# A GNN layer on one core: VectorE's centring moved to the end of its round, odd gathers issued four batches ahead

## Chip, cores and metric

The kernel runs on one core of one Trainium2 chip. The metric is device time in microseconds (us) of one execution, lower is better. Three runs of the kernel before gave a median of 1585.3 us (1584.4 to 1585.63).

## What is computed

One message-passing layer over 100000 nodes of 64 features and 25000 edges, all in fp32. Cut to what matters:

```python
h = jnp.maximum(_layernorm(x, axis=-1), 0.0)
edge_in_f = concat([h[src], h[dst], edge_attr])           # 25000 x 192
msgs_f = relu(edge_in_f @ W1_f + b1_f) @ W2_f + b2_f      # 25000 x 128
agg = segment_sum(msgs_f, dst, n_nodes)
edge_in_r = concat([h[dst], h[src], edge_attr])
msgs_r = relu(edge_in_r @ W1_r + b1_r) @ W2_r + b2_r
agg = agg + segment_sum(msgs_r, src, n_nodes)
out = x + h + relu(concat([agg, h]) @ Wn1 + bn1) @ Wn2 + bn2
```

## The kernel before, in words

There are three stages. The **first** walks over the nodes in 98 windows, normalises them and writes h times a part of Wn1 to a table in HBM. The **third** walks over the same windows, reads the table back and finishes the node MLP. The change touches the **second**, the edge stage.

The edge stage walks over the edges in 98 batches of 256 edges, which have 512 ends, in four groups of 128. For one batch n the work is, in order of data:

- GpSimd *gathers* the rows of x for the four groups (`gather`, L523). Those of even batches are all fetched during the first stage. Those of odd batches go to a ring of four buffers `got_odd`; the first `LOOK` of them (L93) are fetched in the first stage, and the others during the edge stage by `gather_odd` (L543), two of the four groups after each scatter.
- VectorE sums and *centres* the rows (`centre`, L964, instructions at L978 and L980); ScalarE squares them (`square`, L614); VectorE sums the squares (`variance`, L1002); ScalarE takes the root (L619); VectorE scales (`normal`, L1033 and L1037) into `h_ends`.
- TensorE transposes (`turn`, L821 and L824), ScalarE copies the result out (`copy_turned`, L625 and L626), TensorE does `layer1` (L835, L837), ScalarE the `relu` (L633), TensorE `layer2` (L850), and VectorE adds a bias (`messages`, L1028).
- VectorE compares the ends of the batch with one another (`match`, L988 and L996) and works out where each row goes (`targets`, L1008 to L1015, and `aim`, L1022). TensorE sums the messages of equal ends by 20 matmuls (`join`, L863), ScalarE copies these sums out (`copy_sums`, L642).
- GpSimd *scatters* with addition: four indirect DMAs into the table (`scatter`, L541). A scatter starts only when the one before it has landed, when `aim` has written its addresses and when `copy_sums` has written its rows.

Every engine has its own program, a fixed list of steps that it does strictly one after the other; semaphores tie them together. A round n of an engine works on several batches at once. `w.do(f, -2)` means: do f for batch n-2. The lists of ScalarE and TensorE, which the diff leaves alone, are:

```python
# ScalarE, batch(w)
w.do(root)
w.do(relu, -1)
if not fill:
    h_window(w, range(G // 2))
w.do(square, 1)
w.do(copy_sums, -2)
w.do(copy_turned)
# TensorE, batch(w)
w.do(join, -2)
w.do(turn)
w.do(layer2, -1)
w.do(layer1)
```

ScalarE's list ends with the other half of `h_window` (L656), which recomputes h for one window of nodes, beside the edges. GpSimd's round is `scatter` of batch n, then `gather_odd`. `aim` (VectorE, batch n-2) waits until the scatter of batch n-4 has landed, since that scatter still reads the same addresses. The buffers of a step are two, by the parity of the batch.

Of the kernel before, what the change touches and what calls it, by code (L numbers as in the profile page):

```python
# [77 lines left out]
def gnn_layer(nc, x, src, dst, edge_attr, W1_f, b1_f, W2_f, b2_f, W1_r, b1_r, W2_r, b2_r, Wn1, bn1, Wn2, bn2, out):  # L78
# [11 lines left out]
    TB = NT // 2  # L90
    TAIL = E - (NT - 1) * P
    RING = 4
    LOOK = 3  # L93
    PAUSED = 190
    EARLY = 4
    assert NB % 2 == 0 and 0 < TAIL < P and TB < P
# [22 lines left out]
    with ExitStack() as ctx:  # L119
# [177 lines left out]
        def first(i):  # L297
            return isinstance(i, int) and i == 0
# [207 lines left out]
        def _(pool):  # L506
# [14 lines left out]
            def gather(to, numbers, landed, tiles=range(KB)):  # L521
                for k in tiles:
                    pool.indirect_dma_start(to[:, k * D:(k + 1) * D], None, x,  # L523
                                            bass.IndirectOffsetOnAxis(ap=numbers[:, k:k + 1], axis=0)
                                            ).then_inc(landed, 16)
# [18 lines left out]
            def gather_odd(w):  # L544


                pair = w.of(2, 2 * LOOK)[0]
                turn, place = w.of(2 * RING, 2 * LOOK)
                place //= 2
                half = w.n % 2  # L550
                if isinstance(pair, int) and pair < RING:
                    numbers = gather_first[:, (2 * pair + 1) * KB:(2 * pair + 2) * KB]
                else:
                    numbers = gather_at[place]
                    if half == 0:
                        pool.wait_ge(s_gat[place], turn)
                        pool.wait_ge(s_centred[1], pair - RING + 1)
                        pool.sem_inc(s_gathers_begun, 1)
                gather(got_odd[place][:, 0, :], numbers, s_got[place], range(half * JT, (half + 1) * JT))
# [4 lines left out]
            for b in range(NB):  # L564
# [7 lines left out]
                for k in range(KB):  # L572
                    if s == 0:
                        gather(got_even[:, i, :], at, s_got_even[i >= EARLY], [k])
                    elif i < LOOK:
                        gather(got_odd[i][:, 0, :], at, s_got[i], [k])
# [9 lines left out]
            def batch(w):  # L586
                w.do(scatter)
                if w.there(2 * LOOK):
                    gather_odd(w)
# [330 lines left out]
        def _(dve):  # L920
# [35 lines left out]
            def gather_rows(w):  # L956


                place = w.of(2 * RING, 2 * RING)[1] // 2
                dve.tensor_copy(gather_at[place][:, :], gather_first[:, bass.ds(w.number(2 * RING + 1) * KB, KB)]  # L960
                                ).then_inc(s_gat[place], 1)

            def centre(w, k):
                i, s = w.of(2, k)  # L964
                if s == 0:
                    rows = got_even[:, bass.ds(i, 1), :]
                    if first(i):
                        dve.wait_ge(s_got_even[0], 16 * KB * EARLY)
                    elif isinstance(i, int) and i == EARLY:
                        dve.wait_ge(s_got_even[1], 16 * KB * (PAIRS - EARLY))  # L970
                else:
                    turn, place = w.of(2 * RING, k)
                    rows = got_odd[place // 2][:, :, :]
                    dve.wait_ge(s_got[place // 2], 16 * KB * (turn + 1))
                rows = rows.rearrange("p a (k d) -> p (a k) d", d=D)
                if not first(i):
                    dve.wait_ge(s_h[s], i)
                dve.tensor_reduce(sums[s][:, :], rows, AX.X, ALU.add).then_inc(s_sums[s], 1)  # L978
                dve.wait_ge(s_sums[s], i + 1)
                dve.scalar_tensor_tensor(out=centred[s][:, :, :], in0=sums[s][:, :].to_broadcast([P, KB, D]),  # L980
                                         scalar=-1.0 / D, in1=rows, op0=ALU.mult, op1=ALU.add
                                         ).then_inc(s_centred[s], 1)
# [58 lines left out]
            def batch(w):  # L1041
                w.do(variance)
                w.do(aim, -2)
                if w.there(1):
                    centre(w, 1)
                w.do(match, -1)
                w.do(normal)
                if w.n % 2 == 0 and w.there(2 * RING):
                    gather_rows(w)
                w.do(targets, -1)  # L1050
                add_h(w, -1)
                w.do(messages, -1)

            def add_h(w, k):
                if not w.there(k):
                    return
                i, s = w.of(2, k)
                turn, place = w.of(NRING, k)
                dve.wait_ge(e_h[s], i + 1)
                if not in_ring(w, k):  # L1060
                    to = kept_slot(w, k)
                else:
                    to = nxh[place][:, :, :]
                    if not first(turn):
                        dve.wait_ge(e_stored[place], 16 * (turn - skipped(w, k)))
                dve.tensor_tensor(to, nx[place][:, :, :], nh[s][:, :, :], ALU.add).then_inc(e_xh[s], 1)
# [66 lines left out]
            for s in range(2):  # L1133
# [3 lines left out]
                                     in1=all_rstd[:, :, :], op0=ALU.mult, op1=ALU.mult).then_inc(e_means, 1)  # L1137
            assert 2 * EARLY == 8
            run(dve, NB, [(8, MORE_FROM * NRING, 2 * RING), (MORE_FROM * NRING, 88, 2 * RING)], 2, batch)


# [41 lines left out]
```

## Time and profile before

| | |
|---|---|
| median of three runs | 1585.3 us |
| the profiled execution, its own time | 1586.9 us |
| its span, from first to last instruction | 1585.2 us |
| busy: TensorE, VectorE, ScalarE, GpSimd | 1284.4, 972.0, 940.2, 1094.1 us |
| mean granted share of TensorE's full clock | 0.855 |
| first scatter starts, read of the table starts | 331.6 us, 1328.1 us |

The span is what the trace covers; the execution's own time is 1.7 us longer, and the median of the runs 1.6 us shorter than that. In the rows below PE is TensorE, DVE VectorE, ACT ScalarE, POOL GpSimd. A bracket at a row's end gives the idle time before it and what ended it; "issue" there is time in which the engine waited for nothing that the profile shows. The granted clock stands as a share of 2.4 GHz: 1.00 is 2.4 GHz, 0.50 is 1.2 GHz.

### The profile page before, as it was taken

The page shows a single profiled execution, that of the slowest core. Times are in us where ns is not written, and L with a number is a line of the kernel's source. Part 1 is how long each engine was busy: PE and PEld are TensorE (multiplying, and loading weights), DVE is VectorE, ACT ScalarE, POOL GpSimd, SP SyncE. Part 2 cuts the span into 40 slices and gives each one's busy share as a digit, 9 for nine tenths or more (in the row PEclk, how much of TensorE's full clock was granted, in tenths as well). Part 3 has the DMA queues.
Part 4 walks back from the last instruction along what each step waited for, and adds up shares of the span by engine and source line. Part 5 has one row for each costly group of instructions (what it writes and reads, how often), then busy time and mean ns, then how long its engine had stood idle before and what let it go on. Part 6 is the DMA issues. An engine that isn't in the chain of part 4 may idle for free.

```text
span 1585.2 us, 29464 instructions
## 1 busy us (share of the span) xinstructions
PE 1284.4 (81%) x7070; PEld 975.8 (62%) x7070; DVE 972.0 (61%) x3294; ACT 940.2 (59%) x2256; POOL 1094.1 (69%) x985
## 2 busy tenths in 40 slices
PE   5889988747778887787778888777778873999998
PEld 4677777535556666565556666656656652777776
DVE  7999999636666666666666666666666650222222
ACT  4888888635555555545455555555545532777776
POOL 8889878878888888888888888888888863000000
PEclk9999999778887778778887777878887776999999
DMA  6899998535555555555555555555555545999998
GB/s 201 296 315 313 315 313 304 173 60 110 105 110 110 110 105 106 105 105 106 105 99 103 103 103 106 106 105 104 100 104 96 101 91 153 382 371 370 365 363 298
DMA packets 238986, 281.00 MB, mean 177 GB/s; under 512 B 53746, under 2 KB 155776, under 8 KB 238924
## 3 DMA queue, kind: packets, MB, share of 16 engines
q1 hardware_dynamic: 168696, 241.57, 45.7%
q0 software_dynamic: 68992, 38.59, 19.9%
q14 instruction: 57, 0.47, 0.1%
q10 hardware_dynamic: 1236, 0.30, 0.1%
q8 instruction: 5, 0.08, 0.0%
HBM read 162.62 MB, written 117.72 MB: 177 GB/s over the span
## 4 chain that ended last, share of the span: by engine, by line
POOL 54%; issue 24%; PE 18%; DMA 2%; DVE 1%; POOLq 1%; ACT 0%; SPq 0%; DVEq 0%
POOL table L541 30%; POOL got_even L523 13%; POOL got_odd L523 7%; PE bank L888 6%; PE bank L899 6%; POOL to_send L583 4%; PE bank L909 3%; DMA table<-to_send,scatter_at 2%; PE bank L863 1%; PE bank L837 0%; PE bank L835 0%; DVE same L996 0%; PE bank L850 0%; DMA same<-table 0%; DMA gather_begin<-in_src 0%
## 5 line engine op out<-in xcount | busy, mean ns | idle before, releaser
L541 POOL DMA_INDIRECT table<-to_send,scatter_at x392 | 622.2, 1587 | 133.0 <-issue 117.1
L863 PEld LDWEIGHTS bank<-message,same 128*128 128x128 f32 x1960 | 272.3, 224 | 41.9 <-issue 39.5
L863 PE MATMUL bank<-message,same 128*128 128x128 f32 x1960 | 293.2, 315 | 2.2 <-DVE message L1028 2.2
L656 ACT ACTIVATE nh<-nx,all_sums,all_rstd 128x64 f32<-128x64 f32 x784 | 280.1, 433 | 0.0
L523 POOL DMA_INDIRECT got_even<-in_x,gather_first x192 | 207.4, 1080 | 37.7 <-issue 37.7
L821 PE MATMUL bank<-ident,h_ends 128*128 128x128 f32 x196 | 55.0, 376 | 218.0 <-DVE h_ends L1037 218.0
L792 PE MATMUL bank<-wn_h,nturned 128*128 128x256 f32 x784 | 196.0, 393 | 31.3 <-ACT nhidden L700 26.6
L523 POOL DMA_INDIRECT got_odd<-in_x,gather_at x180 | 179.9, 999 | 54.9 <-issue 54.9
L996 DVE TENSOR_SCALAR_CACHE_REDUCE same<-others,ids 128x128 f32<-128x128 int32 (+3 forms) x392 | 190.7, 543 | 12.7 <-DVE ids L988 11.0
L792 PEld LDWEIGHTS bank<-wn_h,nturned 128*128 128x128 f32 x784 | 142.7, 192 | 67.5 <-issue 34.8
L1022 DVE TENSOR_TENSOR scatter_at<-moved,ids 128x4 int32<-128x4 f32 x98 | 15.9, 162 | 265.4 <-DMA table<-to_send,scatter_at 265.4
L835 PE MATMUL bank<-turned,w_ends 128*128 128x256 f32 x392 | 166.8, 516 | 5.0 <-ACT turned_edge L626 5.0
L821 PEld LDWEIGHTS bank<-ident,h_ends 128*128 128x128 f32 x196 | 27.8, 184 | 231.0 <-issue 230.7
L633 ACT ACTIVATE hidden<-bank,b 128x256 f32<-128x256 f32 x196 | 82.0, 469 | 141.4 <-PE bank L837 141.4
L837 PE MATMUL bank<-turned_edge,w_edge 64*128 64x256 f32 x392 | 164.6, 506 | 0.0
L730 ACT ACTIVATE nhidden<-bank,bn_col 128x512 f32<-128x512 f32 x196 | 124.0, 683 | 56.6 <-PE bank L888 56.6
L625 ACT COPY turned<-bank 128x256 f32<-128x256 f32 x98 | 36.5, 373 | 194.3 <-PE bank L824 193.5
L850 PE MATMUL bank<-w2n,hidden 128*128 128x128 f32 x784 | 149.8, 355 | 0.0
L850 PEld LDWEIGHTS bank<-w2n,hidden 128*128 128x128 f32 x784 | 141.4, 269 | 2.1
L888 PE MATMUL bank<-ident,same 128*128 128x128 f32 x784 | 108.6, 282 | 26.0 <-DMA same<-table 25.7
L888 PEld LDWEIGHTS bank<-ident,same 128*128 128x128 f32 x784 | 85.7, 143 | 63.9 <-issue 62.2
L837 PEld LDWEIGHTS bank<-turned_edge,w_edge 64*128 64x128 f32 x392 | 69.2, 220 | 87.7 <-issue 87.7
(81 smaller groups left out, 2012.9 us busy)
## 6 DMA issues: line engine op xcount, KB each, us to landing
nx<-in_x SPq DMA_DIRECT2D x194, 256.0 KB
table<-nhidden SPq DMA_DIRECT2D x97, 512.0 KB
same<-table SPq DMA_DIRECT2D x97, 512.0 KB, 5.3
others<-numbers SPq DMA_DIRECT2D x196, 128.0 KB
out_x<-nh SPq DMA_DIRECT2D x79, 256.0 KB, 4.0
nx<-out_x SPq DMA_DIRECT2D x55, 256.0 KB, 4.3
out_x<-ncentred SPq DMA_DIRECT2D x49, 256.0 KB, 4.3
table<-to_send,scatter_at POOLq DMA_INDIRECT x392
```

The source lines that it names most:

```text
L523: pool.indirect_dma_start(to[:, k * D:(k + 1) * D], None, x, bass.IndirectOffsetOnAxis(ap=numbers[:, k:k + 1], axis=0)).then_inc(landed, 16)
L541: pool.indirect_dma_start(table, bass.IndirectOffsetOnAxis(ap=scatter_at[s][:, k:k + 1], axis=0), to_send[s][:, k, :], None, compute_op=AL ...
L656: last = act.activation(nh[s][:, g, :], nx[place][:, g, :], ACT.Relu, bias=all_sums[:, at, g:g + 1].rearrange("p a g -> p (a g)"), scale=a ...
L730: act.activation(nhidden[s][:, odd * 512:odd * 512 + 512], bank[2 + 2 * s + odd][:, :], ACT.Relu, bias=bn1_col[:, 0:1]).then_inc(n_hidden[ ...
L792: last = pe.matmul(bank[2 + 2 * s + half][:, c:c + 2 * M], nturned[s][:, q * P:(q + 1) * P], wn1_h[:, :, :].rearrange("p a m -> p (a m)"), ...
L835: pe.matmul(bank[2 + s][:, c:c + JT * P], w1_ends[:, end, :], turned[s][:, 0:JT * P], start=True, stop=False)
L837: last = pe.matmul(bank[2 + s][:, c:c + JT * P], w1_edge[:, end, :], turned_edge[s][:, :], start=False, stop=True)
L850: last = pe.matmul(bank[4 + s][:, k * M:(k + 1) * M], hidden[s][:, end, j * P:(j + 1) * P], w2n[:, end, :], start=True, stop=True)
L863: last = pe.matmul(bank[6 + s][:, k * M:(k + 1) * M], same[s][:, o, k * P:(k + 1) * P], message[s][:, o, :], start=(o == k), stop=(o == KB ...
L888: last = pe.transpose(bank[2 + 2 * s + odd][:, q * P:(q + 1) * P], ntab[place][:, g * M:(g + 1) * M], ident[:, :])
L899: last = pe.matmul(bank[s][odd * D:(odd + 1) * D, c:c + 256], wn2[:, :], nhidden[s][:, odd * 512 + c:odd * 512 + c + 256], start=True, sto ...
L996: last = dve.tensor_scalar(same[s][:, o, 0:w], row[:, 0:w], ids[s][:, o:o + 1], None, ALU.is_equal, ALU.add, accum_out=matches[s][:, o:o + 1])
```

## The change

Two edits. In VectorE's round, `centre` of batch n+1 stood right behind `aim`; it now stands at the end, behind `messages` of batch n-1, with `gather_rows` behind it. `gather_rows` copies the indices for a later odd gather to a place where GpSimd may read them. And `LOOK` is 2 instead of 3, so that in round n, with n even, GpSimd begins to gather odd batch n+5 and no longer n+7, and four gathers fewer are done in the first stage.

```diff
-    LOOK = 3
+    LOOK = 2
@@ VectorE
             def batch(w):
                 w.do(variance)
                 w.do(aim, -2)
-                if w.there(1):
-                    centre(w, 1)
                 w.do(match, -1)
                 w.do(normal)
-                if w.n % 2 == 0 and w.there(2 * RING):
-                    gather_rows(w)
                 w.do(targets, -1)
                 add_h(w, -1)
                 w.do(messages, -1)
+                if w.there(1):
+                    centre(w, 1)
+                if w.n % 2 == 0 and w.there(2 * RING):
+                    gather_rows(w)
```

VectorE in the middle of the edge stage, where one round ends and the next begins. L1028 is `messages` of n-1, L1002 `variance` and L1022 `aim` of the next round, L978 and L980 `centre`, L988 the start of `match`; the digit behind a name is its buffer. Before:

```order
L1066 TENSOR_TENSOR nh3<-nx1,nh1 128x512
L1028 TENSOR_TENSOR message1<-bank5,b2n 128x512
L1002 TENSOR_REDUCE var1<-squares1 128x4
L1022 TENSOR_TENSOR scatter_at1<-moved1,ids1 128x4
L978 TENSOR_REDUCE sums0<-got_even 128x4
L980 SCALAR_TENSOR_TENSOR centred0<-sums0,got_even 128x256
L988 COPY ids0<-ends_col 128x4
```

Now:

```order
L1066 TENSOR_TENSOR nh3<-nx1,nh1 128x512
L1028 TENSOR_TENSOR message1<-bank5,b2n 128x512
L978 TENSOR_REDUCE sums1<-got_odd1 128x4
L980 SCALAR_TENSOR_TENSOR centred1<-sums1,got_odd1 128x256
L960 COPY gather_at1<-gather_first 128x4
L1002 TENSOR_REDUCE var1<-squares1 128x4
L1022 TENSOR_TENSOR scatter_at1<-moved1,ids1 128x4
L988 COPY ids0<-ends_col 128x4
```

`centre` has moved ahead of `variance` and `aim` of the next round. Before, the batch that was centred was the one after the batch whose variance stood just ahead; now it is the same batch, with only ScalarE's `square` between them.

GpSimd where the first stage's gathers end and the scatters begin; x18 means 18 such instructions in a row. Before:

```order
L523 DMA got_even<-in_x,gather_first 128x64 x18
L541 DMA table<-to_send0,scatter_at0 100864x128 x4
L523 DMA got_odd3<-in_x,gather_first 128x64 x2
L541 DMA table<-to_send1,scatter_at1 100864x128 x4
L523 DMA got_odd3<-in_x,gather_first 128x64 x2
L541 DMA table<-to_send0,scatter_at0 100864x128 x4
L523 DMA got_odd0<-in_x,gather_at0 128x64 x2
```

Now:

```order
L523 DMA got_even<-in_x,gather_first 128x64 x14
L541 DMA table<-to_send0,scatter_at0 100864x128 x4
L523 DMA got_odd2<-in_x,gather_first 128x64 x2
L541 DMA table<-to_send1,scatter_at1 100864x128 x4
L523 DMA got_odd2<-in_x,gather_first 128x64 x2
L541 DMA table<-to_send0,scatter_at0 100864x128 x4
L523 DMA got_odd3<-in_x,gather_first 128x64 x2
```

Four gathers have left the run ahead of the first scatter, and every later pair of gathers is for an odd batch two batches nearer.

## Rows read from the trace of the kernel before

**Rows 1.** Busy us by stretch: PE, PEld, DVE, ACT, POOL; granted clock, DMA share, GB/s
```profile
341.00:1276.00 935.00, 740.19 (x3677) 566.44 (x3678) 602.08 (x2526) 485.58 (x1380) 766.70 (x551) 0.80 0.55 105
...
607.10:620.30 13.20, 12.13 (x44) 9.41 (x45) 9.17 (x43) 5.16 (x15) 10.76 (x9) 0.50 0.61 112
```

**Rows 2.** Timeline of GpSimd, one batch: start us, us, what
```profile
808.67 1.63 POOL L541 DMA_INDIRECT table<-to_send,scatter_at  x1 [0.30 <-issue]
...
816.22 1.02 POOL L523 DMA_INDIRECT got_odd<-in_x,gather_at  x1 [0.31 <-issue]
...
818.82 1.62 POOL L541 DMA_INDIRECT table<-to_send,scatter_at  x1 [0.30 <-issue]
```

**Rows 3.** Timeline of VectorE about the same time
```profile
804.26 0.69 DVE L1028 TENSOR_TENSOR message<-bank,b2n 128x512 f32<-128x512 f32 x1 [0.81 <-PE bank L850]
...
807.45 0.16 DVE L1022 TENSOR_TENSOR scatter_at<-moved,ids 128x4 int32<-128x4 f32 x1 [2.17 <-DMA table<-to_send,scatter_at]
807.53 0.42 DVE L978 TENSOR_REDUCE sums<-got_odd 128x4 f32<-128x256 f32 x1
807.98 0.42 DVE L980 SCALAR_TENSOR_TENSOR centred<-sums,got_odd 128x256 f32<-128x256 f32 x1
```

**Rows 4.** Timeline of ScalarE about the same time
```profile
808.99 0.41 ACT L614 ACTIVATE squares<-centred 128x256 f32<-128x256 f32 x1
809.44 0.58 ACT L642 COPY to_send<-bank 128x512 f32<-128x512 f32 x1
811.87 0.37 ACT L625 COPY turned<-bank 128x256 f32<-128x256 f32 x1 [1.84 <-PE bank L824]
812.14 0.36 ACT L626 COPY turned_edge<-bank 64x256 f32<-64x256 f32 x1
```

**Rows 5.** Timeline of TensorE, a batch at 2.4 GHz
```profile
811.20 0.41 PE L821 MATMUL bank<-ident,h_ends 128*128 128x128 f32 x2 [1.88 <-DVE h_ends L1037]
...
811.67 1.06 PE L850 MATMUL bank<-w2n,hidden 128*128 128x128 f32 x8
812.56 0.69 PE L835 MATMUL bank<-turned,w_ends 128*128 128x256 f32 x2
...
815.06 2.50 PE L863 MATMUL bank<-message,same 128*128 128x128 f32 x20
```

**Rows 6.** Timeline of TensorE, a batch at 1.2 GHz and the start of the next
```profile
609.05 1.92 PE L850 MATMUL bank<-w2n,hidden 128*128 128x128 f32 x8
610.76 1.06 PE L835 MATMUL bank<-turned,w_ends 128*128 128x256 f32 x2
...
615.20 4.63 PE L863 MATMUL bank<-message,same 128*128 128x128 f32 x20
619.62 0.63 PE L821 MATMUL bank<-ident,h_ends 128*128 128x128 f32 x2
...
620.48 1.08 PE L850 MATMUL bank<-w2n,hidden 128*128 128x128 f32 x8
```

**Rows 7.** Timeline of TensorE, two resumptions at 1.2 GHz behind a pause
```profile
309.91 1.22 PE L835 MATMUL bank<-turned,w_ends 128*128 128x256 f32 x2 [4.29 <-ACT turned_edge L626]
...
699.87 0.66 PE L821 MATMUL bank<-ident,h_ends 128*128 128x128 f32 x2 [2.89 <-DVE h_ends L1037]
```

**Rows 8.** Instructions and DMAs of the tile got_odd
```profile
DMA to landing us min/median/max: 2.3/2.5/5.8
```

**Rows 9.** Timeline of GpSimd: last early gather, first scatter, first scatter of batch 93
```profile
330.35 0.95 POOL L523 DMA_INDIRECT got_even<-in_x,gather_first  x1 [0.31 <-issue]
331.61 1.62 POOL L541 DMA_INDIRECT table<-to_send,scatter_at  x1 [0.30 <-issue]
...
1278.00 1.63 POOL L541 DMA_INDIRECT table<-to_send,scatter_at  x1 [2.62 <-DMA table<-to_send,scatter_at]
```

**Rows 10.** Timeline of VectorE: it reaches the wait for the first landing
```profile
340.54 0.16 DVE L1022 TENSOR_TENSOR scatter_at<-moved,ids 128x4 int32<-128x4 f32 x1 [18.47 <-DMA table<-to_send,scatter_at]
```

**Rows 11.** Who waited for whom, GpSimd, 341 to 1276 us: total us, times, longest
```profile
POOL table L541 <- ACT to_send L642: 0.9, 3, 0.3
```

## The prediction

> **What bounds the kernel now.** I read the engines by stretch first. In the edge stage, 341 to 1276 us, GpSimd is busy for 766.70 of 935 us and TensorE for 740.19, at a mean granted clock of 0.80 [rows 1]. So busy time alone doesn't tell who sets the pace; the waits do. GpSimd's timeline shows a batch of four scatters, from 808.67, and two gathers, from 816.22, and the next scatter at 818.82, 10.15 us after the first, with nothing ahead of it but 0.30 us of issue [rows 2]. Its waits in the whole stretch hold only 0.9 us for ScalarE's copy of the sums [rows 11]. So GpSimd's own list of instructions is the bound: from the first scatter at 331.61 to that of batch 93 at 1278.00 it makes (1278.00 - 331.61) / 93 = 10.18 us a batch [rows 9]. VectorE, ScalarE and TensorE run ahead and are held back at one place, VectorE's `aim`, which waits for a scatter to land: 2.17 us at 807.45 [rows 3].
>
> TensorE's work for one batch depends on its clock. At 2.4 GHz `layer1` takes 812.56 to 815.06 = 2.50 us, `join` 2.50, `turn` 811.20 to 811.67 = 0.47, `layer2` 1.06 [rows 5]: 6.53. At 1.2 GHz `layer1` takes 4.44 (610.76 to 615.20), `join` 4.42 (to the next turn at 619.62), `turn` 0.86, `layer2` 1.92 [rows 6]: 11.64, which is longer than GpSimd's batch. Today this does no harm: a low stretch as that of 607.10 to 620.30, with clock 0.50 [rows 1], is made up in the next batch. That the wait for ScalarE's copy shows up at all [rows 11] says that little is left over.
>
> **The change, part by part.** *Four gathers leave the start.* They stood in the run of unpaused gathers right ahead of the first scatter, 330.35 to 331.61 = 1.26 us each [rows 9]. The first scatter starts 4 x 1.26 = 5.0 us sooner, at 326.6. The same four come back in two more rounds of the edge stage, two each, 2.60 us [rows 2]; there they stand beside a wait for the landing that without them takes 2.62 us [rows 9]. That is 0 on the path, and if the cover were missing, 5.2 us. Sum: -5.0.
>
> *The copy of indices* (`gather_rows`, one small copy every second round) is moved with `centre`. GpSimd reads its result four rounds later instead of two, so its cost is nothing, covered by these rounds; uncovered it would be that small copy alone.
>
> *`centre` goes behind `messages`.* This adds no instruction, but it closes a ring. `messages` of batch m-1 waits for `layer2` of m-1. ScalarE's `square` of m+1 now waits for that, and behind `square` in ScalarE's fixed list stand `copy_sums` of m-2 and `copy_turned` of m. `layer1` of m needs `copy_turned` of m; in TensorE's list `join` of m-1, `turn` of m+1 and `layer2` of m follow, and `layer2` of m lets `messages` of m go. One turn of the ring is one batch, and nobody in it can run ahead. Before, `centre` needed nothing of TensorE's current batch, so `copy_turned` ran as soon as `turn` was done.
>
> Off TensorE the ring has: `messages` 0.69, `centre` 807.53 to 808.40 = 0.87 [rows 3], `square` to the start of the copy 0.45, `copy_sums` 0.58, `copy_turned` 811.87 to 812.50 = 0.63 [rows 4]. Sum 3.22. In this time TensorE does nothing. On TensorE the ring has all its work, in the order `layer1`, `join`, `turn`, `layer2`:
> - wholly at 2.4 GHz: 6.53 + 3.22 = 9.75 us, below GpSimd's 10.18;
> - wholly at 1.2 GHz: 11.64 + 3.22 = 14.86 us;
> - `layer1` and `join` at 1.2 GHz, `layer2` at 2.4: 4.44 + 4.42 + 1.06 + 3.22 = 13.14, and a `turn` of 0.47 to 0.86: 13.6 to 14.0.
>
> I take the third. The reason is the rows on the clock. TensorE resumed at 1.2 GHz after pauses of 2.89 and of 4.29 us [rows 7], and the new order puts a pause of 3.22 into each batch. The one at 309.91 is the new order's own case: the pause ended with `copy_turned`, and `layer1` came first. Once low, `layer1` and `join` stay low: in 24 batches of the trace the last three pairs of `layer1`'s matmuls ran at 1.2 GHz, and in 21 of these the whole `join` did; the clock rose in the next `turn` or `layer2`, as at 620.48 with 1.08 us instead of 1.92 [rows 6]. Before, `turn` and `layer2` came first after a pause and the clock was mostly back by `layer1`. Listed ends on one engine overlap the next start by some 0.1 us (0.37 listed, 0.27 to the next [rows 4]), so I take 13.7 and keep 13.3 to 14.0.
>
> *Odd gathers come two batches later.* Before, the rows of an odd batch were gathered ahead of one more batch of scatters (7.55 us [rows 2]) than the landing that `centre` stood behind, and were there in time. Now `centre` of odd batch m needs the second pair of gathers behind scatter m-4, and that scatter needs `copy_sums` of m-4, which ScalarE does right behind `square` of m-1. So from `centre` of m-1 to `centre` of m it takes at least: 0.87 + 0.45 + 0.58, scatters 808.67 to 816.22 = 7.55, one gather issued 1.30 (half of 2.60) [rows 2], and the second one's landing 2.5 [rows 8]: 13.25 us. The trace shows landings of 2.3 to 5.8 [rows 8], so the bounds are 13.05 and 16.55; the median is the nearest to a usual one. Even batches have no such wait. At 13.7 this is hidden behind the first ring, by only 0.45 us; a landing over 3.0 us would show.
>
> **The sum.** VectorE is free until its first wait for a landing [rows 10], which is `aim` of batch 2, in round 4. From round 4 to 96 are 93 rounds: 93 x (13.7 - 10.18) = 327.4 us. At the end GpSimd no longer trails its inputs by a batch, which gives back 0 to 10 us: -5. With the -5.0 from above: +317.4. The node stages have nothing changed. Against the profiled execution's own 1586.9 us this is 1904.3; the median of the runs shown is 1.6 lower: **1902.7, I say 1902 us**.
>
> **The rivals.** *The clock holds, the gathers bind* (0.22, with all mixtures up to 13.2 us a batch). If TensorE stays at 2.4 GHz, its ring of 9.75 is harmless, but odd batches take 13.25 and even ones 10.18: 11.7 on the mean. 93 x 1.54 = 143 us, less 5, from 1585.3: 1723 us. For it: TensorE would be busy for 6.53 of 9.75, and pauses of 1.88 us didn't lower the clock [rows 5]. Against it: 2.89 us did [rows 7], and 3.22 is longer.
>
> The Trainium skill's page "TensorE: Matmul & The Clock Gate", section "HAM oscillation — how this bites in real kernels", gives a length of idle gap up to which the clock isn't lowered, and 3.22 lies below it. By that rule this rival would be the outcome, 1723 us instead of 1902. The pause of 2.89 with 1.2 GHz behind it disagrees, so I leave it at 0.22.
>
> *All at 1.2 GHz, or late landings* (0.13). At 14.86 us a batch: 93 x 4.68 = 435, less 10: 2010 us; from 14.1 on it would be 1940. Against it: in the trace `layer2` was mostly back at 2.4 after a low `join`.
>
> *GpSimd keeps its pace* (0.05, of which 0.03 faster and 0.02 the same). If both rings close within 10.18 us, only the -5.0 is left: 1580.3 us, faster. The place is `centre` of the odd batches; the point from which it decides is a turn below 10.18, that is a landing some 3 us earlier than the 2.5 measured [rows 8] or rows fetched sooner than the code says, and a clock that holds. The order of GpSimd's instructions speaks against that.
>
> **How the numbers follow.** The forecast, 13.3 to 14.0 us a batch, 1865 to 1930 us, has 0.60. The range of 8 in 10 takes in most of the first rival, whose single value 1723 is its bottom, and the lower part of the second: 1720 to 1965. About 0.2% is what a measurement of this kernel can tell from no change; slower by more than that is 0.60 + 0.22 + 0.13 = 0.95, the same 0.02, faster 0.03.
>
> **What would show it.** In the changed kernel's profile: VectorE's wait of `aim` for the scatter's landing almost gone, and GpSimd waiting for ScalarE's `to_send`, some 3 us a batch; one pause a batch on TensorE, ahead of L835 and ended by `turned_edge`, of about 3.2 us, and none ahead of L821; granted clock in the edge stage near 0.65 instead of 0.80; L863 near 4.6 us in nearly every batch; the first scatter near 326.6. If instead the clock is high and GpSimd's scatters come 10.2 and 13.3 us apart in turn, the first rival holds. It is wrong altogether if the scatters keep 10.18 us.

## The result, and the profile after

The changed kernel took 1905.6 us (median of four runs, 1902.8 to 1906.4), the kernel before 1585.5 us beside it: a ratio of 1.2016 (95% interval 1.1995 to 1.2037), slower by 320 us. The prediction said 1902 us, with 1720 to 1965.

Of the changed kernel's page, the busy times, the granted clock in 40 slices, and the two costliest lines of GpSimd and TensorE:

```profile
span 1904.7 us, 29474 instructions
PE 1447.5 (76%) x7070; PEld 1089.5 (57%) x7070; DVE 975.1 (51%) x3294; ACT 923.7 (48%) x2256; POOL 1100.4 (58%) x985
...
PEclk9999996667766767676767676767666766799999
...
L541 POOL DMA_INDIRECT table<-to_send,scatter_at x392 | 629.4, 1606 | 447.5 <-ACT to_send L642 352.2
L835 PE MATMUL bank<-turned,w_ends 128*128 128x256 f32 x392 | 195.4, 592 | 381.1 <-ACT turned_edge L626 381.1
```

VectorE, ScalarE and GpSimd have the same work as before (1100.4 us of GpSimd against 1094.1); what is new is idle time. The scatters, which in [rows 2] waited for nothing but issue, now wait 352.2 us for ScalarE's copy of the sums. TensorE waits 381.1 us ahead of `layer1`.

The engines by stretch, columns as in [rows 1], and below it the longest waits in the same kernel, 500 to 1200 us (us in total, times, longest):

```profile
336.00:1590.00 1254.00, 888.40 (x3644) 670.09 (x3645) 600.68 (x2512) 464.40 (x1365) 773.60 (x552) 0.69 0.42 78
```

```profile
ACT squares L614 <- DVE centred L980: 310.1, 51, 7.9
DVE message L1028 <- PE bank L850: 263.2, 51, 5.9
...
PE bank L835 <- ACT turned_edge L626: 202.4, 52, 6.7
POOL table L541 <- ACT to_send L642: 192.8, 52, 4.7
...
DVE sums L978 <- DMA got_odd<-in_x,gather_at: 43.0, 26, 3.6
```

This is the ring, read off by its waits: `messages` waits for `layer2`, `square` for `centre`, `layer1` for `copy_turned`, each once a batch (51 or 52 times in 700 us). The wait of `aim` for a landing, 265.4 us in the kernel before by its page, is no longer in the list. The last line is the second ring, the wait of `centre` for a gather, every second batch. The mean granted clock in the edge stage fell from 0.80 to 0.69.

GpSimd's timeline, the first of the four scatters, at the stage's start, four times in its middle, and of batch 93:

```profile
324.58 1.63 POOL L541 DMA_INDIRECT table<-to_send,scatter_at  x1 [0.30 <-issue]
...
801.03 1.62 POOL L541 DMA_INDIRECT table<-to_send,scatter_at  x1 [3.05 <-ACT to_send L642]
...
814.97 1.63 POOL L541 DMA_INDIRECT table<-to_send,scatter_at  x1 [4.12 <-ACT to_send L642]
...
828.18 1.63 POOL L541 DMA_INDIRECT table<-to_send,scatter_at  x1 [2.87 <-ACT to_send L642]
...
1594.78 1.63 POOL L541 DMA_INDIRECT table<-to_send,scatter_at  x1 [4.24 <-ACT to_send L642]
```

From 324.58 to 1594.78 are 93 batches: 13.66 us each, against 10.18 before [rows 9]. The batches are not alike: the three scatters in the middle are 13.94 and 13.21 us apart. Over the stage the first scatter of an even batch comes 14.13 us behind that of the odd one before it, and that of an odd batch 13.20 us behind the even one's. Where the 319.5 us of span went: 1270.20 - 946.39 = 323.8 in these batches, -7.0 at the start (331.61 to 324.58), +2.7 behind batch 93.

TensorE in the same two turns of the ring, which are unlike in the same way:

```profile
800.62 0.70 PE L835 MATMUL bank<-turned,w_ends 128*128 128x256 f32 x2 [3.02 <-ACT turned_edge L626]
...
803.86 4.63 PE L863 MATMUL bank<-message,same 128*128 128x128 f32 x20
808.29 0.63 PE L821 MATMUL bank<-ident,h_ends 128*128 128x128 f32 x2
...
814.72 1.22 PE L835 MATMUL bank<-turned,w_ends 128*128 128x256 f32 x2 [4.56 <-ACT turned_edge L626]
...
819.32 4.10 PE L863 MATMUL bank<-message,same 128*128 128x128 f32 x20
823.26 0.38 PE L821 MATMUL bank<-ident,h_ends 128*128 128x128 f32 x2
...
827.77 0.70 PE L835 MATMUL bank<-turned,w_ends 128*128 128x256 f32 x2 [3.02 <-ACT turned_edge L626]
```

Behind a pause of 3.02 us `layer1` begins at 2.4 GHz (0.70 for a pair of matmuls) and the clock falls within it; behind 4.56 us it runs at 1.2 GHz from its start (1.22), and the clock is back before the join ends (4.10 instead of 4.63).

### The profile page after: what moved, and what is told of

The parts are those of the page before. It is cut to its first block, busy times and chain, and to the rows that moved or that the text cites. A ratio compares the mean times of both kernels' runs of the same rounds, so it can differ in the third digit from the quotient of the medians.

```text
span 1904.7 us, 29474 instructions
## 1 busy us (share of the span) xinstructions
PE 1447.5 (76%) x7070; PEld 1089.5 (57%) x7070; DVE 975.1 (51%) x3294; ACT 923.7 (48%) x2256; POOL 1100.4 (58%) x985
## 4 chain that ended last, share of the span: by engine, by line
PE 38%; issue 17%; POOL 17%; DVE 12%; DMA 9%; ACT 4%; ACTq 1%; DVEq 1%; SPq 1%; POOLq 0%
POOL table L541 14%; PE bank L863 10%; DMA got_odd<-in_x,gather_at 6%; PE bank L835 6%; PE bank L837 6%; PE bank L888 5%; PE bank L899 5%; DVE nvar L1087 3%; POOL got_odd L523 2%; PE bank L850 2%; PE bank L909 2%; DVE centred L980 2%; DVE sums L978 2%; DVE ncentred L1081 2%; ACT to_send L642 2%
## 5 line engine op out<-in xcount | busy, mean ns | idle before, releaser
L541 POOL DMA_INDIRECT table<-to_send,scatter_at x392 | 629.4, 1606 | 447.5 <-ACT to_send L642 352.2
L835 PE MATMUL bank<-turned,w_ends 128*128 128x256 f32 x392 | 195.4, 592 | 381.1 <-ACT turned_edge L626 381.1
L863 PEld LDWEIGHTS bank<-message,same 128*128 128x128 f32 x1960 | 399.4, 313 | 63.6 <-issue 62.7
L863 PE MATMUL bank<-message,same 128*128 128x128 f32 x1960 | 422.9, 407 | 0.8 <-DVE message L1028 0.8
L835 PEld LDWEIGHTS bank<-turned,w_ends 128*128 128x128 f32 x392 | 79.9, 254 | 449.4 <-ACT turned_edge L626 400.0
L614 ACT ACTIVATE squares<-centred 128x256 f32<-128x256 f32 x98 | 40.8, 416 | 589.5 <-DVE centred L980 589.5
L1028 DVE TENSOR_TENSOR message<-bank,b2n 128x512 f32<-128x512 f32 x98 | 67.7, 691 | 501.6 <-PE bank L850 501.6
L837 PE MATMUL bank<-turned_edge,w_edge 64*128 64x256 f32 x392 | 214.2, 643 | 0.0
L1008 DVE CUSTOM_DVE_ANT_0 junk<-same,from_here,matches 128x128 bf16<-128x128 f32 x392 | 114.0, 346 | 0.0
L850 PE MATMUL bank<-w2n,hidden 128*128 128x128 f32 x784 | 109.4, 284 | 0.0
L700 ACT COPY nhidden<-bank 128x512 f32<-128x512 f32 x196 | 105.3, 593 | 7.4 <-DMA table<-nhidden 7.3
```

What stands on the lines that cost most here:

```text
L541: pool.indirect_dma_start(table, bass.IndirectOffsetOnAxis(ap=scatter_at[s][:, k:k + 1], axis=0), to_send[s][:, k, :], None, compute_op=AL ...
L835: pe.matmul(bank[2 + s][:, c:c + JT * P], w1_ends[:, end, :], turned[s][:, 0:JT * P], start=True, stop=False)
L837: last = pe.matmul(bank[2 + s][:, c:c + JT * P], w1_edge[:, end, :], turned_edge[s][:, :], start=False, stop=True)
L850: last = pe.matmul(bank[4 + s][:, k * M:(k + 1) * M], hidden[s][:, end, j * P:(j + 1) * P], w2n[:, end, :], start=True, stop=True)
L863: last = pe.matmul(bank[6 + s][:, k * M:(k + 1) * M], same[s][:, o, k * P:(k + 1) * P], message[s][:, o, :], start=(o == k), stop=(o == KB ...
L1008: last = dve.tensor_tensor_reduce(junk[s][:, k, :], same[s][:, k, k * P:(k + 1) * P], from_here[:, :], -1.0, matches[s][:, k:k + 1], ALU.m ...
```

## The experiments

All are compared with the kernel before on the same chip (1583.9 to 1585.6 us). Where no interval is given the time is of one run; differences of hundreds of us need no more, and the 9 us by which some runs stand above the kernel before are to be held against its own runs, which lay between 1581.5 and 1586.6 us. "Per batch" is the mean from the first scatter to that of batch 93.

| run | VectorE's order | LOOK | also | us | per batch |
|---|---|---|---|---|---|
| before | old | 3 | | 1585 | 10.18 |
| changed | new | 2 | | 1905.6 | 13.66 |
| e1 | new | 3 | | 1901.7 | 13.56 |
| e2 | old | 2 | | 1838.9 | 12.87 |
| e3 | new | 2 | square late | 1595.1 | 10.33 |
| e4 | new | 3 | filler | 1594.4 | 10.29 |
| e5 | new | 2 | filler | 1868.3 | 13.22 |
| e6 | centre ahead of messages | 3 | | 1594.3 | 10.26 |
| e7 | new | 3 | square late | 1594.4 | 10.27 |
| e8 | old | 2 | square late | 1860.8 | 13.14 |
| e9 | old | 3 | filler | 1593.7 | 10.28 |
| e10 | new | 3 | copy_sums last | 1901.4 | 13.54 |
| e11 | old | 3 | 150 pauses | 1575.3 | 10.15 |
| e12 | old | 3 | 110 pauses | 1568.3 | 10.16 |

### The order alone, and the gathers alone

e1 undoes one part of the change, e2 the other:

```diff
-    LOOK = 2
+    LOOK = 3
```

> VectorE's new order alone; LOOK stays 3, so odd gathers are six batches ahead as before. Theory A (the ring messages, centre, square, copy_sums, copy_turned, layer1, join, turn, layer2, slow because TensorE runs most of it at 1.2 GHz): 13.0 to 13.7 us a batch, 1850 to 1905 us, granted clock in the edge stage 0.65 to 0.70, no wait of centre for a gather. Theory B (the nearer gathers are the cause): back at 1585 us.

Measured: 1901.7 us, 13.56 us a batch. Theory B falls: with the old gathers the time is all but the same. Theory A's pace holds (13.0 to 13.7); the clock of 0.62 lies a little below its 0.65 to 0.70. It is also the cleanest sight of the first ring. TensorE in e1, one turn of it, and the clock of 700 us:

```profile
812.64 1.22 PE L835 MATMUL bank<-turned,w_ends 128*128 128x256 f32 x2 [3.02 <-ACT turned_edge L626]
813.79 1.22 PE L837 MATMUL bank<-turned_edge,w_edge 64*128 64x256 f32 x2
...
817.24 4.63 PE L863 MATMUL bank<-message,same 128*128 128x128 f32 x20
821.67 0.50 PE L821 MATMUL bank<-ident,h_ends 128*128 128x128 f32 x2
...
822.22 1.06 PE L850 MATMUL bank<-w2n,hidden 128*128 128x128 f32 x8
826.29 1.22 PE L835 MATMUL bank<-turned,w_ends 128*128 128x256 f32 x2 [3.02 <-ACT turned_edge L626]
```

```profile
500.00:1200.00 700.00, 546.13 (x2048) 401.75 (x2049) 335.94 (x1418) 260.80 (x767) 432.26 (x309) 0.62 0.43 77
```

From 812.64 to 826.29 are 13.65 us. After a pause of 3.02 us `layer1` (4.60 us to the join's start) and the whole `join` ran at 1.2 GHz, `layer2` (1.06) at 2.4, and the clock rose in the `turn` (0.50 for its first part, between the 0.41 and the 0.63 of [rows 5] and [rows 6]): the case that the prediction chose. 96 of its 98 joins took over 4.5 us.

e2 is the kernel before with `LOOK = 2` and nothing else.

> LOOK 2 alone; VectorE's order as before. Theory A says that the gathers make a ring of their own (centre of an odd batch waits for a gather, square behind it holds copy_sums, and copy_sums holds the scatter ahead of the next gathers): odd batches 13 to 14 us, even ones near 10.2, on the mean 11.7 to 12, 1725 to 1770 us. Theory C (gathers still hidden, only the order matters): 1580 to 1586 us.

Measured: 1838.9 us, 254 us slower than before, and 69 us beyond the upper end of what I had expected. So the gathers are not harmless either. From scatter to scatter it takes 14.0 us behind an odd batch, as expected, but 11.8 behind an even one, expected at 10.2; no run takes the second apart. The two parts don't add up (317 and 254 against 320 together): both rings have a turn of about the same length, 13.6 us (e1) and 14.0 (e2, every second batch), and whichever is longer hides the other. VectorE in e2, where an odd batch is centred:

```profile
815.52 0.42 DVE L978 TENSOR_REDUCE sums<-got_odd 128x4 f32<-128x256 f32 x1 [6.98 <-DMA got_odd<-in_x,gather_at]
815.97 0.42 DVE L980 SCALAR_TENSOR_TENSOR centred<-sums,got_odd 128x256 f32<-128x256 f32 x1
816.32 0.16 DVE L988 COPY ids<-ends_col 128x4 f32 x1
```

It waits 6.98 us at the head of its round, with `match`, `normal` and `messages` behind it. My expectation had the wait reach the scatter only by way of ScalarE. e8 asks for the way:

```diff
# e2, and on ScalarE
-                w.do(square, 1)
                 w.do(copy_sums, -2)
                 w.do(copy_turned)
+                w.do(square, 1)
```

> e2_look_only (VectorE's order as before, LOOK 2) with ScalarE's square behind its two copies. Theory A1 (in e2 the wait for a gather reaches the scatter through square and copy_sums on ScalarE): the scatters are free again, 1580 to 1600 us. Theory A2 (it reaches it through VectorE, where centre stands ahead of match, normal and messages and holds them all): no better than e2_look_only, 1740 to 1850 us.

Measured: 1860.8 us, not better than e2, and 11 us above the upper end of what I expected. With ScalarE's copies free of `square`, the wait still reaches the scatters: theory A1 falls, and what is left is A2, the way by VectorE's list. That way was not opened by a run of its own.

### Opening the rings

e3 has the same edit on ScalarE, in the changed kernel.

> The changed kernel, with ScalarE's square moved behind copy_sums and copy_turned. This takes ScalarE's copies out of both rings, and nothing else. Theory A: both rings are open, GpSimd's list is the bound again at 10.2 us a batch, and the 5 us of the earlier first scatter stay: 1575 to 1590 us. Theory D (TensorE's low clock or the landing of the gathers alone is enough, whatever ScalarE's order): over 1700 us.

Measured: 1595.1 us, ratio to before 1.0069 (1.0052 to 1.0085), 10.33 us a batch. Three steps in another order on an engine that is busy for half the time take 310 us off the changed kernel. Theory D falls for the gathers: their distance alone costs little, as long as a late `centre` holds up nothing but its own batch. For the clock e3 says less, since it was back at 0.81 from 500 to 1200 us, as in the kernel before (0.80). VectorE still waits for gathers in e3 (140.9 us from 500 to 1200), now at the end of its round, and the scatters wait for almost nothing:

```profile
L541 POOL DMA_INDIRECT table<-to_send,scatter_at x272 | 433.2, 1593 | 85.3 <-issue 82.3 <-DMA table<-to_send,scatter_at 2.8 <-ACT to_send L642 0.3
```

The result is 5 us above the upper end of what I expected; more on this below.

e6 opens the first ring at another joint (LOOK 3):

```diff
+                if w.there(1):
+                    centre(w, 1)
+                if w.n % 2 == 0 and w.there(2 * RING):
+                    gather_rows(w)
                 w.do(messages, -1)
-                if w.there(1):
-                    centre(w, 1)
-                if w.n % 2 == 0 and w.there(2 * RING):
-                    gather_rows(w)
```

> As e1_order_only (LOOK 3), with centre one step earlier, ahead of messages instead of behind it. Theory A: the ring is closed by messages' wait for layer2; ahead of it centre depends on nothing of TensorE's current batch, so the time is back at 1583 to 1595 us. Theory F (it is centre standing late in the round, behind targets and the window's addition, that delays everything): still over 1800 us.

Measured: 1594.3 us. One place up in VectorE's list makes 307 us. `centre` is still late in the round, behind 4.9 us of other work (803.00 to 807.90), so lateness is not the cause; standing behind the wait for `layer2` is.

### The clock

e4 fills TensorE's pause, with e1's order otherwise:

```diff
# TensorE
+            def filler(i, s):
+                for _ in range(9):
+                    pe.matmul(bank[1 - s][D:2 * D, 2 * P:4 * P], wn2[:, :],
+                              w2n[:, :, :].rearrange("p a m -> p (a m)"), start=True, stop=True)
+
                 w.do(layer2, -1)
+                w.do(filler)
                 w.do(layer1)
```

> As e1_order_only, with nine extra matmuls of 256 columns a batch on TensorE between layer2 and layer1, 0.31 us each at 2.4 GHz, into a part of a bank that nobody reads. They fill the pause of some 3 us. Theory A: the clock stays at 2.4 GHz (1.00 in nearly all of the edge stage), the ring takes 9.8 us and GpSimd's 10.18 is the bound: 1585 to 1600 us. Theory E (the ring is too long at any clock, the low clock is a by-product): no faster than e1_order_only, 1850 us or more.

Measured: 1594.4 us, against 1901.7 without the filler. Here nothing was reordered; TensorE only got more to do, 18 more pieces a batch, and the kernel is 307 us faster:

```profile
500.00:1200.00 700.00, 700.00 (x3944) 489.68 (x3943) 454.36 (x1870) 347.27 (x1020) 574.41 (x408) 1.00 0.54 103
```

TensorE is busy all 700 us at a granted clock of 1.00. The low clock is what makes the ring the bound, and the ring's own pause is what lowers the clock. Theory E falls. The ring itself can't be timed here, and the 9.75 us of the prediction stay a sum: the nine matmuls took 4.10 us (L869 in e5's rows below) where I had expected 9 x 0.31 = 2.8, so they more than fill the pause, and TensorE's own list makes 10.30 us a batch (596.93 to 607.23, from one `layer1` to the next). That, without any idle time, is e4's pace.

e9 has the same filler in the kernel before.

> The kernel before, with nine extra matmuls a batch on TensorE. It tells what the clock is worth where no ring is closed. Theory A: TensorE has slack there at either level, so a clock near 1.00 in the edge stage gains nothing: 1583 to 1595 us, GpSimd at 10.2 us a batch. If a higher clock speeds up the kernel before too (under 1580 us), the low clock was a cost of its own and the filler runs say less about the ring.

Measured: 1593.7 us, no gain. From 500 to 1200 us:

```profile
500.00:1200.00 700.00, 700.00 (x3945) 489.66 (x3944) 439.32 (x1870) 346.50 (x1020) 575.66 (x409) 1.00 0.55 103
```

This run says less than it was meant to. TensorE has no idle time here either, and the filler makes its list 10.30 us long, more than the 10.18 of the kernel before, so the run could not have become faster. It shows that the filler by itself costs 10 us and gains none. That TensorE's clock is worth nothing where no ring is closed rests on the kernel before: its scatters do not wait for what TensorE feeds (ScalarE's copy of a batch's sums ended 4.6 us or more ahead of that batch's first scatter), at a clock of 0.80.

e5 has the filler in the changed kernel, LOOK 2.

> The changed kernel with the same nine extra matmuls a batch on TensorE. Where the filler keeps TensorE at 2.4 GHz, theory A leaves the gather ring alone: odd batches 13.3 to 14 us, even ones 10.2, on the mean 11.8 to 12.1 and 1725 to 1765 us, as e2_look_only was meant to be. But a wait for a gather can make the pause longer than the filler; if the clock then falls again, the time stays at 1850 to 1905 us. Theory E (clock a by-product) also says 1850 or more, but with a granted clock near 1.00.

Measured: 1868.3 us, granted clock 0.89 from 500 to 1200 us. The second of the outcomes named: where VectorE waits for a gather, the pause outlasts the filler. TensorE in e5; L869 is the filler, and the batch that begins at 810.86 ends in a wait:

```profile
810.86 0.70 PE L835 MATMUL bank<-turned,w_ends 128*128 128x256 f32 x2
...
816.15 1.06 PE L850 MATMUL bank<-w2n,hidden 128*128 128x128 f32 x8
817.13 4.10 PE L869 MATMUL bank<-w2n,wn 128*64 128x256 f32 x18
824.54 0.70 PE L835 MATMUL bank<-turned,w_ends 128*128 128x256 f32 x2 [3.31 <-ACT turned_edge L626]
825.17 1.22 PE L837 MATMUL bank<-turned_edge,w_edge 64*128 64x256 f32 x2
```

So the rival "clock holds, 11.7 us a batch" was not reached even with help: an even batch's scatter came 14.2 us behind the one before, as in the changed kernel, and an odd one's 12.3.

e10 shortens the first ring without opening it (e1, ScalarE's `copy_turned` ahead of `copy_sums`).

> As e1_order_only, with ScalarE's copy_turned ahead of copy_sums, which takes the 0.5 to 0.6 us of copy_sums out of the ring and leaves the rest of it. Theory A: the turn of the ring shortens by at least those 0.5 us of e1's 13.56 us, to 13.0 or less, and by more where the shorter pause spares some of the 1.2 GHz; 93 x 0.5 = 47 us, so 1855 us or less, down to 1775. If copy_sums isn't in the ring, the time stays at 1900.

Measured: 1901.4 us, a miss. TensorE in e10:

```profile
809.06 1.22 PE L835 MATMUL bank<-turned,w_ends 128*128 128x256 f32 x2 [2.54 <-ACT turned_edge L626]
...
818.09 0.64 PE L821 MATMUL bank<-ident,h_ends 128*128 128x128 f32 x2
...
818.94 1.24 PE L850 MATMUL bank<-w2n,hidden 128*128 128x128 f32 x8
822.72 1.22 PE L835 MATMUL bank<-turned,w_ends 128*128 128x256 f32 x2 [2.54 <-ACT turned_edge L626]
```

The pause did shrink by 0.48 us, from 3.02 to 2.54, so `copy_sums` is in the ring. But `turn` and `layer2` take as much longer (818.09 to 820.18, against 821.67 to 823.28 in e1): the clock comes back later, and the turn is 13.66 us again. The saved half microsecond was spent at 1.2 GHz.

### What 10 us are left, and a faster kernel

e7 is e3 with LOOK 3.

> VectorE's new order, LOOK 3, and ScalarE's square behind its two copies. Both rings open and no gather two batches nearer: 1583 to 1595 us; against e3_square_late it tells whether the 10 us that e3 lacks come with LOOK 2 (then 1585 here) or with the orders (then 1593 or more here).

Measured: 1594.4 us, the second of the two outcomes. The missing 10 us do not come with the nearer gathers: these may account for 10.33 us a batch in e3 against 10.27 here, which e3's earlier first scatter makes up. e4, e6, e7 and e9 all end at 1594 us, with 10.26 to 10.29 us a batch, but not for one reason. In e4 and e9 TensorE's list, with the filler, is 10.30 us long and TensorE is never idle. (GpSimd shows no wait in e9 either, with 1611 ns for a scatter; whether its instructions are longer by themselves there can't be told.) In e6 and e7 TensorE has idle time and GpSimd waits for nothing; there its own instructions take longer. GpSimd in e7, 500 to 1200 us (busy, mean ns of one):

```profile
L541 POOL DMA_INDIRECT table<-to_send,scatter_at x273 | 441.2, 1616 | 83.2 <-issue 82.9 <-ACT to_send L642 0.3
```

In the kernel before this mean is 1583 ns over the same stretch. 4 x 33 ns x 93 batches = 12 us, where the kernel is 9 us slower. It is not that every scatter is slower: the medians are 1586 and 1573 ns, and most of the difference stands in the third scatter of a batch (1668 ns on the mean against 1564), of which a few take up to 2.07 us, as the one at 786.33 with 2.03 us. In e3 the scatters take 1593 ns and the gathers 1051 instead of 999. Why is open: such scatters of over 2 us occur also in the changed kernel and in e1 and not at all in e10, which differs from e1 only in the order of two copies on ScalarE.

The change's one gain was the earlier first scatter. e11 buys it without touching the rings. The first stage puts a memset behind each of the first 190 gathers, to hold them back:

```diff
# the kernel before
-    PAUSED = 190
+    PAUSED = 150
```

> The kernel before, with 150 pauses between the first stage's gathers instead of 190 and nothing else. The change gained 5 to 7 us by starting the scatters sooner, and lost them many times over. Here the same start is had otherwise: a paused gather takes 1.45 us and an unpaused one 1.26, 40 x 0.19 = 7.6 us, if the denser gathers don't slow down the first stage: 1577 to 1581 us, faster than both kernels. If the first stage, which shares the DMA engines, is slowed by as much: 1585 us.

Measured: 1575.3 us, ratio 0.9945 (0.9929 to 0.9962): half a per cent faster than the kernel before, clear of the interval, and a little more than expected. The first scatter moved by 9.7 us, and e12 goes on to 110.

> As e11_fewer_pauses, with 110 pauses. Going from 190 to 150 moved the first scatter from 331.6 to 321.9 us and the time by 8.6 us. If a start of the scatters is worth its own length as long as the addresses and the rows of the first batch are ready (near 302 us in e11), 40 pauses less again give 8 to 10 us: first scatter near 312 us, 1565 to 1568 us. If the denser gathers now slow down the first stage, 1572 us or more.

Measured: 1568.3 us, ratio 0.9894 (0.9878 to 0.9911), at the upper end of what was expected. GpSimd's first scatter in e11, then in e12:

```profile
321.92 1.62 POOL L541 DMA_INDIRECT table<-to_send,scatter_at  x1 [0.30 <-issue]
```

```profile
313.40 1.63 POOL L541 DMA_INDIRECT table<-to_send,scatter_at  x1 [0.30 <-issue]
```

From 190 to 110 pauses the first scatter comes 18.2 us sooner and the kernel is 17 us faster; the pace of 10.16 us stays. Where GpSimd is the bound from end to end, its start is worth nearly its full length. Fewer than 110 weren't tried.

## Why the prediction was right, point by point

- **GpSimd is the bound before**: right. e11 and e12 turn its start into time nearly one for one. One reading on the way was wrong: the 0.9 us of waits for ScalarE's copy [rows 11] was taken for a sign that little is left over. These are three waits of 0.30 us, as long as an issue, and they stand ahead of the third scatter of a batch whose sums had been copied 13 us before. From the end of a batch's copy to its first scatter the least was 4.6 us and the median 9.1: there was much to spare. Nothing in the sum hangs on it.
- **A ring closes through messages, centre, square and ScalarE's copies**: shown three ways. Taking `centre` from behind `messages` (e6), taking `square` from in front of the copies (e7, and e3 for the change itself), and raising the clock (e4) each bring 1901.7 us back to 1594.
- **The third case of the clock, 13.7 us a turn**: right, and for the reason given in e1, which has only this ring and makes 13.56 us; the changed kernel makes 13.66. In the changed kernel itself the picture is mixed: 47 joins took over 4.5 us, 49 between 3 and 4.5, so "L863 near 4.6 us in nearly every batch" holds for e1 (96 of 98) and not for the change, and the clock was 0.69, not 0.65. That this case would come was less certain than the chosen rows made it look. Two pauses of the kernel before, ten us apart:

```profile
689.37 0.66 PE L821 MATMUL bank<-ident,h_ends 128*128 128x128 f32 x2 [3.43 <-DVE h_ends L1037]
...
694.48 2.50 PE L863 MATMUL bank<-message,same 128*128 128x128 f32 x20
699.87 0.66 PE L821 MATMUL bank<-ident,h_ends 128*128 128x128 f32 x2 [2.89 <-DVE h_ends L1037]
...
706.89 4.63 PE L863 MATMUL bank<-message,same 128*128 128x128 f32 x20
```

  Behind the longer pause the clock was back before the join, behind the shorter one it was not. The rows that the prediction chose all had the long low stretch behind them.
- **The gathers are hidden by 0.45 us**: this step failed. VectorE waited for them 45 times, 79.6 us in total, for example in the first of the two turns shown above:

```profile
812.34 0.42 DVE L978 TENSOR_REDUCE sums<-got_odd 128x4 f32<-128x256 f32 x1 [1.45 <-DMA got_odd<-in_x,gather_at]
```

  The landing was as forecast, a median of 2.5 us. What was missing in the sum of 13.25 is the hand-over from ScalarE's copy to GpSimd: ScalarE's rows and GpSimd's row of the changed kernel are

```profile
799.47 0.57 ACT L642 COPY to_send<-bank 128x512 f32<-128x512 f32 x1
```

```profile
801.03 1.62 POOL L541 DMA_INDIRECT table<-to_send,scatter_at  x1 [3.05 <-ACT to_send L642]
```

  The copy ends at 800.04, and the scatter starts 0.99 us later. With it the turn of an odd `centre` is 13.25 + 0.99 = 14.2 us, and 14.13 was measured, from an odd batch's scatter to the next even one's. That the mean still came out at 13.7 is luck. The other turn measured 13.20 instead of 13.7: from 814.72 to 827.77 `layer1` is wholly at 1.2 GHz (4.60 us to the join), but the clock is back during the join, so that join and `turn` take 4.38 us (819.32 to 823.70) where e1's take 4.98 (817.24 to 822.22). The 2.4 GHz at the head of `layer1` in the turn from 800.62 gains nothing, since that turn waits for the gather.
- **The start, -5.0 us**: it was -7.0. **The end, -5**: it was +2.7. The pace gave 323.8 us instead of 327.4. Three errors of -3.6, -2.0 and +7.7 us almost cancel; that 1902 stands within 4 us of 1905.6 is luck too.
- **The rival of the page's rule** (the clock holds at pauses of about 3.2 us, 1723 us): the granted clock says no. Pauses of 3.02 us in e1 and 2.54 us in e10 were followed by 1.2 GHz in every turn shown, and behind 3.02 us in the changed kernel the clock held at first and fell within `layer1`. The Trainium skill's page "TensorE: Matmul & The Clock Gate", section "HAM oscillation — how this bites in real kernels", gives a length of gap below which this shouldn't happen; here the measurement decides. The 1723 us were too low as well, by the same missing hand-over: with 14.2 instead of 13.25 us for every second batch the mean is 12.2, and 93 x 2.03 - 5 above 1585.3 gives an estimate of 1769 us. No run had the changed gathers at a clock of 1.00; e5, at 0.89, made 1868.
- **Slower by more than 0.2%**: right, at a chance of 0.95.

## What to carry to other kernels

Before moving a step behind a wait, follow what stands behind it on the *next* engine's list: here `square`, which had been free, came to stand between a wait and the very copies that the waited-for engine needed, and an order that looked like a shift of 0.9 us of work became a ring through four engines. Sum such a ring at both clock levels: with the clock held at 2.4 GHz it fitted into 10.3 us (e4), with the clock that its own pause brought about it took 13.6 (e1). In such a sum count the hand-over from one engine to the next too: the 0.99 us left out here turned a margin of 0.45 us into a wait. When an experiment adds work to an engine, check that this engine doesn't become the bound, as it did in e4 and e9. And two changes that each close a ring of their own hide one another, so test them one at a time.

## What was unexpected of the hardware

- Pauses of TensorE of 2.54 us, once in 13.66 us, were enough to have the next 9 us at 1.2 GHz (e10). Nine dummy matmuls in each pause held 2.4 GHz and made the kernel 307 us faster (e4).
- Making the ring 0.48 us shorter gained nothing: the turn stayed at 13.65 us (e1) and 13.66 us (e10), because the clock rose that much later.
- A scatter that had to wait for ScalarE started 0.8 to 1.0 us after the copy's end (800.04 to 801.03, 814.15 to 814.97). So did the first scatters of 94 of the 98 batches of the changed kernel.
- GpSimd's scatter instructions took 1582 to 1616 ns on the mean from run to run, by a few long ones of up to 2.07 us; 2% of them, on the engine that is the bound, is about 10 us. What makes them long is open.
- Pauses of 3.43 and 2.89 us, ten us apart in one trace, were followed by 2.8 us and by 12.8 us at 1.2 GHz (689.37 to 692.19, 699.87 to 712.67, by the granted clock of the kernel before): the length of a pause alone didn't tell how long the clock stayed low.
